# Message layers of a graph network: the node update's gate made inside the layer, its squares on ScalarE, its products last

## The reference

```python
def _block(h, src, dst, w, wm, bm, gm, bem, wu, bu, gu, beu, wg, bg):
    ecat = jnp.concatenate([h[src], h[dst]], axis=-1)
    em = jax.nn.relu(_layernorm(ecat @ wm.T + bm, gm, bem)) * w[:, None]
    msum = jax.ops.segment_sum(em, dst, num_segments=n)
    ...
    messages = msum / (cnt + 1e-08) * valid
    tw = jax.nn.sigmoid(h @ wg.T + bg)
    h_new = jax.nn.relu(_layernorm(jnp.concatenate([h, messages], axis=-1) @ wu.T + bu, gu, beu))
    return tw * h_new + (1 - tw) * h
```

## Time and profile before

| | us |
|---|---|
| median of 3 runs | 8488.0 (8477.32 to 8499.33) |
| profiled execution, its time | 8487.61 |
| profiled execution, its span | 8485.4 |
| busy: TensorE, VectorE, ScalarE, GpSimd | 5608.4, 3945.3, 3333.3, 4632.2 |

### The profile page before, as it was taken

The page is one execution under the profiler, slowest core; times in us unless marked ns, Lnnn a source line. Parts: engine busy times, 40 slices in busy tenths (PEclk is TensorE's granted clock), DMA queues, the critical chain, the costliest instruction groups (busy, mean ns, idle before and its releaser), DMA issues.

```text
span 8485.4 us, 124245 instructions
## 1 busy us (share of the span) xinstructions
PE 5608.4 (66%) x35700; PEld 4994.7 (59%) x35700; DVE 3945.3 (46%) x13716; ACT 3333.3 (39%) x12502; POOL 4632.2 (55%) x4868
## 2 busy tenths in 40 slices
PE   7445545577777667776757776675767775677676
PEld 5333333567666656666646666664666664666666
DVE  4221221456666556665653444452444443444445
ACT  2222221366666556666623333332333332333332
POOL 2555554366666356666526666535666663666662
PEclk9999999899999888888867888887888887888887
DMA  2011000334344234444313333333333332333332
GB/s 56 22 25 25 22 24 19 98 103 104 103 103 104 67 97 121 119 121 116 106 41 107 108 107 105 106 88 83 107 106 106 108 107 69 106 109 107 108 110 66
DMA packets 489685, 743.91 MB, mean 88 GB/s; under 512 B 219285, under 2 KB 351865, under 8 KB 487973
## 3 DMA queue, kind: packets, MB, share of 16 engines
q1 hardware_dynamic: 307764, 423.98, 16.0%
q0 software_dynamic: 180928, 305.59, 15.0%
q10 hardware_dynamic: 320, 6.40, 0.3%
HBM read 636.97 MB, written 97.83 MB: 87 GB/s over the span
## 4 chain that ended last, share of the span: by engine, by line
PE 20%; issue 14%; DVE 12%; another core or an unknown queue 12%; ACT 4%; DVEq 3%; ACTq 0%; POOL 0%; DMA 0%
PE PS L1355 5%; DVE AR L1943 5%; PE PS L1369 4%; PE PS L1245 2%; PE PS L1367 2%; PE PS L1269 2%; PE PS L1266 2%; DVEq L507 1%; ACT AR L1042 1%; DVE AR L1864 1%; PE PS L1380 1%; DVEq L1943 1%; DVE AR L1789 1%; ACT AR L1031 1%
## 5 line engine op out<-in xcount | busy, mean ns | idle before, releaser
L579 POOL DMA_INDIRECT AR<-gtab_d,AR x2436 | 2304.7, 946 | 1536.9 <-issue 606.2
L571 POOL DMA_INDIRECT AR<-ptab_d,AR x1624 | 1544.9, 951 | 1038.8 <-issue 394.1
L1042 ACT ACTIVATE AR<-PS,AR 128x512 f32<-128x512 f32 x609 | 418.2, 687 | 2533.9 <-remote 1286.9
L1355 PE MATMUL PS<-AR 128*112 128x132 f32 x4872 | 939.9, 334 | 673.3 <-DVE AR L1943 651.4
L1355 PEld LDWEIGHTS PS<-AR 128*112 128x112 f32 x4872 | 736.8, 211 | 819.0 <-DVE AR L1943 511.2
L1943 DVE TENSOR_TENSOR AR<-AR,PS 112x132 f32 x2436 | 696.1, 286 | 1002.3 <-issue 356.8
L553 POOL DMA_INDIRECT rec_d<-AR x782 | 756.9, 968 | 670.4 <-DVE AR L1550 446.4
L1369 PE MATMUL PS<-AR 128*128 128x128 f32 x4872 | 1051.8, 318 | 18.4 <-issue 18.2
L2020 DVE SCALAR_TENSOR_TENSOR AR<-PS,AR 128x512 f32<-128x512 f32 x609 | 455.7, 748 | 1211.9 <-issue 654.2
L1369 PEld LDWEIGHTS PS<-AR 128*128 128x128 f32 x4872 | 920.5, 235 | 20.6 <-issue 20.4
L1245 PE MATMUL PS<-AR 128*112 128x161 f32 x3248 | 667.9, 333 | 361.4 <-DVE AR L1864 218.4
(11 more groups left out here) (342 smaller groups left out, 8859.4 us busy)
## 6 DMA issues: line engine op xcount, KB each, us to landing
AR<-ste_d SPq DMA_DIRECT2D x404, 512.0 KB
AR<-nbb_d SPq DMA_DIRECT2D x303, 224.0 KB
ste_d<-AR SPq DMA_DIRECT2D x101, 512.0 KB
AR<-gtab_d,AR POOLq DMA_INDIRECT x2436
AR<-ptab_d,AR POOLq DMA_INDIRECT x1624
nbb_d<-AR SPq DMA_DIRECT2D x101, 224.0 KB
AR<-key_d SPq DMA_DIRECT2D x94, 224.0 KB
AR<-rec_d SPq DMA_DIRECT2D x812, 8.0 KB
```

The costliest lines, as they stand in the source:

```text
L571: e.indirect_dma_start(out=XJ1[:, t % 32, :], out_offset=None, in_=tabs_d[0][:, :], in_offset=off).then_inc(done_, 16)
L579: e.indirect_dma_start(out=xj2(t)[:, t % 4, :], out_offset=None, in_=tabs_d[1][:, :], in_offset=off).then_inc(done_, 16)
L1355: x = e.matmul(PS[6 + v_ % 2][0:B, (t % 2) * 132:(t % 2 + 1) * 132], SQ4[:, i % 4, t % 4, :], PX[:, i % 5, t % 4, :, :].rearrange("p c h - ...
```

## The change

- **Gate inside the layer.** `GATES` is the quad of the last own block plus 4 (169, 180). There ScalarE takes one exponential over all 28 blocks' gate columns of `Z`; two quads later VectorE makes the gate `tw33` and `n33` = 1 - gate; from four quads later on ScalarE multiplies `H` in place by 1 - gate, two blocks in each quad.
- **Update.** VectorE combines 160 columns instead of 161 (`updated`). ScalarE squares each block with an accumulator (`squares`) and takes the quarter's root (`update_root`). `mixed(l, q)`: reciprocal, times gate, seven instructions (times scale times gain), seven (plus bias times gate), one pass (clip and add the gated old features).
- **Order.** TensorE: updated 0 to 3, then products 0 to 3. ScalarE: the same, with squares of quarters 0, 1, 2, 3 beside updated 1, updated 2, products 0, products 1, and in layer 1 all row roots behind the last product. VectorE: updated 0, updated 1, mixed 0, updated 2, mixed 1, updated 3, mixed 2, mixed 3, then all `rows_out`.

```diff
 OWN = [{30 + 5 * b: b for b in range(NB)}, {122 + 2 * b: b for b in range(NB)}]
+
+GATES = [max(o) + 4 for o in OWN]
...
+                    if j == GATES[l]:
+                        w.wait_ge(s_dve, DV[f"own{l}"])
+                        done(e.activation(tw33, Z[:, :, D], ACT.Exp, scale=-1.0), s_act)
+                    lo = 2 * (j - GATES[l] - 4)
+                    if 0 <= lo < NB:
+                        w.wait_ge(s_dve, DV[f"om{l}"])
+                        for b in (lo, lo + 1):
+                            x = e.activation(H[:, b, :], H[:, b, :], ACT.Copy, scale=n33[:, b:b + 1])
+                        if lo + 2 == NB:
+                            done(x, s_act)
...
-                def roots(q):
-                    lo = q * CH
-                    done(root(ssq33[:, lo:lo + CH], 1.0 / D, f"us{l}_{q}"), s_act)
-                    tc = tw33[:, lo:lo + CH]
-                    done(e.activation(tc, U[:, lo:lo + CH, D], ACT.Exp, scale=-1.0), s_act)
...
-                def updated(q, norm_of=None, roots_of=None):
-                    for k in range(CH):
-                        sums_turned(q * CH + k)
-                        if k == 2 and roots_of is not None:
-                            roots(roots_of)
-                        if l == 1 and norm_of is not None:
-                            if k == 2:
-                                norm_root(norm_of)
-                            if k == 5:
-                                row_root(norm_of)
+                def squares(q, k):
+                    b = q * CH + k
+                    w.wait_ge(s_dve, DV[f"us{l}_{q}"])
+                    done(e.activation(SQ[:, b, :], U[:, b, 0:D], ACT.Square, accum_out=ssq33[:, b:b + 1]))
+
+                def update_root(q):
+                    x = ssq33[:, q * CH:(q + 1) * CH]
+                    w.wait_own()
+                    done(e.activation(x, x, ACT.Sqrt, bias=eps[0:B, :], scale=1.0 / D), s_act)
...
-                        done(e.activation(Z[:, q * CH + k, 0:n], PS[(2, 2, 2, 5)[q] + BANK[k]][0:B, PLACE[k] * n:(PLACE[k] + 1) * n], ACT.Copy), s_aev)
...
+                        done(e.activation(Z[:, q * CH + k, 0:n], PS[(2, 5, 2, 5)[q] + BANK[k]][0:B, PLACE[k] * n:(PLACE[k] + 1) * n], ACT.Copy), s_aev)
...
+                def with_squares(turn, q, of, k0):
                     for k in range(CH):
-                        b = q * CH + k
-                        turn_block("tab1" if l == 0 else "out", b, b % 2, HT1, HT2, True)
-                        if k == 4:
-                            products_out(q, (0, 1, 2))
-                            if roots_of is not None:
-                                roots(roots_of)
-                        if l == 1 and norm_of is not None:
-                            if k == 2:
-                                norm_root(norm_of)
-                            if k == 5:
-                                row_root(norm_of)
-                    products_out(q, (3, 4))
-                    products_out(q, (5, 6))
-
-                updated(0)
-                updated(1, roots_of=0)
-                products(0, roots_of=1)
-                updated(2, norm_of=0)
-                products(1, roots_of=2)
-                updated(3, norm_of=1)
-                products(2, roots_of=3)
-                products(3, norm_of=2)
+                        turn(q, k)
+                        if of is not None and k >= k0:
+                            squares(of, k - k0)
+                    if of is not None:
+                        for k in range(CH - k0, CH):
+                            squares(of, k)
+                        update_root(of)
+
+                def updated(q, k):
+                    sums_turned(q * CH + k)
+
+                def products(q, k):
+                    b = q * CH + k
+                    turn_block("tab1" if l == 0 else "out", b, b % 2, HT1, HT2, True)
+                    if k == 4:
+                        products_out(q, (0, 1, 2))
+                    if k == 6:
+                        products_out(q, (3, 4))
+                        products_out(q, (5, 6))
+
+                with_squares(updated, 0, None, 0)
+                with_squares(updated, 1, 0, 2)
+                with_squares(updated, 2, 1, 2)
+                with_squares(updated, 3, None, 0)
+                with_squares(products, 0, 2, 0)
+                with_squares(products, 1, 3, 2)
+                with_squares(products, 2, None, 0)
+                with_squares(products, 3, None, 0)
                 if l == 1:
-                    norm_root(3)
-                    row_root(3)
+                    for q in range(4):
+                        x = n33[:, q * CH:(q + 1) * CH]
+                        w.wait_ge(s_dve, DV[f"on{q}"])
+                        done(e.activation(x, x, ACT.Sqrt), s_act)
+                        done(root(ssq33[:, q * CH:(q + 1) * CH], 1.0 / 128, f"x{q}_0"), s_act)
...
                 updated(0, 2)
                 updated(1, 5)
                 w.wait_ge(s_dve, DV[f"us{l}_0"])
+                updated(2, 2)
+                w.wait_ge(s_dve, DV[f"us{l}_1"])
+                updated(3, 5)
+                w.wait_ge(s_dve, DV[f"us{l}_2"])
                 products(0, 2)
-                w.wait_ge(s_dve, DV[f"us{l}_1"])
-                updated(2, 5)
+                w.wait_ge(s_dve, DV[f"us{l}_3"])
+                products(1, 5)
                 w.wait_ge(s_aev, aev_at(p, CH - 1))
-                products(1, 2)
-                w.wait_ge(s_dve, DV[f"us{l}_2"])
-                updated(3, 5)
+                products(2, 2)
                 w.wait_ge(s_aev, aev_at(p, 2 * CH - 1))
-                products(2, 2)
-                w.wait_ge(s_dve, DV[f"us{l}_3"])
                 products(3, 5)
...
-            def update(l, q):
+            def updated(l, q):
 
                 lo = q * CH
-                Uz, Hc, tc = U[:, lo:lo + CH, 0:D], H[:, lo:lo + CH, :], tw33[:, lo:lo + CH]
-                w.wait_own()
                 for ks in ((0, 1, 2), (3, 4), (5, 6)):
                     w.wait_ge(s_mmu, sum_at(l, lo + ks[-1]))
                     for k in ks:
                         b = lo + k
-                        v(e.scalar_tensor_tensor(U[:, b, :], PS[(2, 5, 5, 5)[q] + BANK[k]][0:B, PLACE[k] * 161:(PLACE[k] + 1) * 161],
-                                                 CR[:, b:b + 1], Z[:, b, :], ALU.mult, ALU.add))
-                w.wait_own()
-                sumsq(Uz, SQ[:, lo:lo + CH, :], ssq33[:, lo:lo + CH], f"us{l}_{q}")
-                inverse(ssq33[:, lo:lo + CH], f"us{l}_{q}")
-                w.wait_ge(s_act, AC[f"tw{l}_{q}"])
-                v(e.tensor_scalar(tc, tc, 1.0, None, ALU.add))
-                w.wait_own()
-                v(e.reciprocal(tc, tc))
-                w.wait_own()
-                v(e.tensor_tensor(Uz, Uz, each(ssq33, lo, D), ALU.mult))
-                w.wait_own()
-                v(e.tensor_tensor(Uz, Uz, over(guB), ALU.mult))
-                w.wait_own()
-                v(e.tensor_tensor(Uz, Uz, over(beuB), ALU.add))
-                w.wait_own()
-                v(e.scalar_tensor_tensor(Uz, Uz, 0.0, Hc, ALU.max, ALU.subtract))
-                w.wait_own()
-                v(e.tensor_tensor(Uz, Uz, each(tw33, lo, D), ALU.mult))
-                w.wait_own()
-                mile(e.tensor_tensor(Hc, Hc, Uz, ALU.add), f"h{l}_{q}")
+                        x = e.scalar_tensor_tensor(U[:, b, 0:D], PS[(2, 5, 2, 5)[q] + BANK[k]][0:B, PLACE[k] * 161:PLACE[k] * 161 + D],
+                                                   CR[:, b:b + 1], Z[:, b, 0:D], ALU.mult, ALU.add)
+                        if k == 6:
+                            mile(x, f"us{l}_{q}")
+                        else:
+                            v(x)
+
+            def mixed(l, q):
+
+                lo = q * CH
+                Uz, Hc, sc = U[:, lo:lo + CH, 0:D], H[:, lo:lo + CH, :], ssq33[:, lo:lo + CH]
+                inverse(sc, f"us{l}_{q}")
+                v(e.tensor_tensor(sc, sc, tw33[:, lo:lo + CH], ALU.mult))
+                w.wait_own()
+                for b in range(lo, lo + CH):
+                    v(e.scalar_tensor_tensor(U[:, b, 0:D], U[:, b, 0:D], ssq33[:, b:b + 1], guB, ALU.mult, ALU.mult))
+                for b in range(lo, lo + CH):
+                    w.wait_ge(s_vown, w.count[s_vown.name] - CH + 1)
+                    v(e.scalar_tensor_tensor(U[:, b, 0:D], beuB, tw33[:, b:b + 1], U[:, b, 0:D], ALU.mult, ALU.add))
+                w.wait_own()
+                w.wait_ge(s_act, AC[f"hs{l}"])
+                mile(e.scalar_tensor_tensor(Hc, Uz, 0.0, Hc, ALU.max, ALU.add), f"h{l}_{q}")
...
+                    if j == GATES[l] + 2:
+                        w.wait_ge(s_act, AC[f"tw{l}"])
+                        v(e.tensor_scalar(tw33, tw33, 1.0, None, ALU.add))
+                        w.wait_own()
+                        v(e.reciprocal(tw33, tw33))
+                        w.wait_own()
```

(22 more changed lines are left out.)

18 lines of the change are left out of this document (7 added, 11 removed), and 4 rows, old and new, of the table DV.

## The result

| | before | changed |
|---|---|---|
| median of 5 runs, us | 8488.0 (8477.32 to 8499.33) | 8436.19 (8427.01 to 8441.27) |
| profiled execution, its time and span, us | 8487.61, 8485.4 | 8427.01, 8424.8 |
| busy: TensorE, VectorE, ScalarE, GpSimd, us | 5608.4, 3945.3, 3333.3, 4632.2 | 5601.5, 3907.3, 3352.0, 4643.3 |

The account below looks back on a forecast made before the run. Layers paced by gathers and slot return, updates by the order of TensorE, ScalarE and VectorE. Gains 27.6 (layer 0) + 22.2 (layer 1) - 1.2 (uncovered copies) = 48.6 us; 8487.6 - 48.6 = 8439.0 us, range 8410 to 8466.

Parts of the forecast that it names:

- Update 0: Layer 0's update, TensorE's first turn to last product copied out: 55.2 us instead of 82.8, a gain of 27.6 us.
- Update 1: Layer 1's update, TensorE's first turn to last output row: 98.6 us instead of 120.8, a gain of 22.2 us.
- The wait: Update of layer 1: VectorE stands some 4.3 us for the first row root, which ScalarE gives only behind all products.
- the term that carries layer 0's times over: Layer 1's update starts 1389.8 us after layer 0's, same steps; 128-column products save 0.4; quarter 3's features at 4294.7.
- Squares on ScalarE: Both updates: a square with accumulator costs 0.42 to 0.5 us, hidden by TensorE's own 0.74 us a block.
- The tail of layer 1: From 4211.6 ScalarE runs without a gap; gated copies of quads 196 and 197 lie there and cost 1.2 us.
- The stall at the start of layer 1: Behind layer 0's update TensorE is busy 8.7 of 43 us; gather 1 to gather 33 stays 71 us.
- rivals 3, 4 and 5: In order, stall after updates: takes gain back, 8488 us, chance 0.09; doubles, 8525, chance 0.04; shrinks by half, 8396, chance 0.07.
- Rival 1: Message layers pay for the work moved into them, 25 us if cover fails everywhere: 24.8 us gained, 8463; chance 0.10.
- rival 2: VectorE's block instructions in the updates are dear: 8442 us in its small form, 8462 at 0.6 us each; chance 0.05.
- rival 6: ScalarE becomes the updates' limit at 1 us a block instead of 0.71, 7 us more a layer: 8453; chance 0.10.
- A sign of being wrong that came true: In the update, VectorE idle between its quarters longer than 2 us after the second would show the forecast wrong.

Follow-up runs that it names:

- the two copies a quad: Changed kernel with two extra 128x160 ScalarE copies in each of quads 20 to 159 of both message layers; 8362.2 us (one run), changed kernel beside it 8372.4.
- the kernel with whole passes: Changed kernel with VectorE's 14 block instructions of a quarter made as four passes over the whole quarter; 8451.7 us (one run).

## Why the prediction was right

- **Update 0, 27.6 us forecast, 28.0 measured.** Its steps held too. New part of a quarter 5.95, measured 6.0 (block instruction 0.29 taken, 0.297 found). Roots of quarters 2 and 3 ready 34.7 and 42.5 us after the first turn, measured 34.2 and 41.9. Features 48.6, measured 48.0. Last products 6.6, measured 6.8.
- **Update 1, 22.2 forecast, 24.5 measured.** The wait (4.3 against 4.20) and the rows (11.53 against 11.58 a quarter) were right. Mis-sized is the term that carries layer 0's times over: features came 4255.13-4209.11 = 46.0 us after the first turn, not 48.2. That term holds a clock: the sums of the first quarter, some 42 matmuls, take 8.6 us in update 0 at a granted clock of 0.65, 7.5 in update 1 at 0.77, and 6.0 in the one trace in which update 0 ran at 1.00 from the start. Behind them the clock is 1.00 up to the features in all three, and the rest takes 39.4, 38.6 and 39.4 us. So of the 2.2 us about 1.1 are the clock, which was not forecast: luck. Another 0.6 is layer 0's own (48.0 for 48.6). The last 0.4 lies behind the first quarter, where layer 1 was 0.8 shorter and 0.4 was taken for its narrower products; what made it twice as much is not shown.
- **Squares on ScalarE**, 0.42 to 0.5 forecast: 0.44 in a block, 0.32 from start to start in a row. Hidden, as said; on VectorE they cost 6 us a layer as built.
- **The layers pay little or nothing** (at most the 2 to 3 us of one comparison). A gated copy takes 0.413 us and a pair 0.73, where 0.31 and 0.62 were worked out, and it didn't matter, because the cover is 2.2 us a quad. The tail of layer 1, from the last wait of ScalarE to the first turn, grew from 34.91 to 35.54 us: 0.6, not 1.2.
- **The stall at the start of layer 1** stayed (71.4 to 70.3 us), so rivals 3, 4 and 5 fell with the changed kernel's trace. Rival 1 fell with the two copies a quad, rival 2 with 0.297, rival 6 with 0.75 us a block.
- **A sign of being wrong that came true:** I named idle time of VectorE between its quarters of more than 2 us after the second. It was 2.85 us ahead of quarter 2's root. The mechanism doesn't fall with it, for my own sum held a longer wait: quarter 0 done at 2877.3, then 2.14, 5.95 and 2.14 us of work, and the root at 2891.4 leave about 3.9 us. The sign was drawn tighter than the sum.
- **Slips that carried no weight:** 3.65 us for a root is quarter 1's wait alone; the others waited 0.37, 1.24 and 1.25. The sums end at 2883.4 by the terms given, not 2883.6. The row of 348 ns set beside 324 ns is one of 128 elements, not 160. Behind the wait for the first row root stand 43.6 us of rows by the sum itself, not 46.
- **Where the reading was wrong without harm:** I said that a layer is paced by its gathers and the loop that gives back their slots. TensorE's waits over the middle of layer 0, kernel before and changed kernel, and then over the like stretch of the kernel with squares on VectorE, on the other chip:

```profile
PE PS L1229 <- issue: 133.7, 77, 3.2
...
PE PS L1234 <- issue: 137.4, 77, 3.1
PE PS L1234 <- DVE AR L1793: 13.5, 9, 3.1
```

```profile
PE PS L1270 <- DMA AR<-ptab_d,AR: 64.0, 103, 1.8
PE PS L1230 <- DVE AR L1788: 6.8, 14, 0.9
```

  In 600 us TensorE stood 133.7 and 137.4 us ahead of one line for nothing the profile names, and GpSimd waited for it; on the other chip that idle time is gone, TensorE waits for the gathers, and these come every 1.27 us. So in the forecast's traces TensorE's unexplained waits held back the gathers. The conclusion that ScalarE has room stood on its own idle time, and that was right.

## What to carry to other kernels

- In a stage where three engines hand work round, shortening the work and loosening the order are no separate gains. Either alone moved the bound to the other (71 and 74 us of 83); both together took 28 us off. Forecast them as one schedule, from the first instruction to the last, and not as a sum.
- Work that needs no result of a stage belongs ahead of it, where another resource sets the pace. How much fits is at most the idle time of that engine in a cycle (here 2.2 us of 6), and a few dummy instructions measure it: 0.7 us went in free, of 2.66 only some 1.5.
- When work is moved behind everything else, look at what then waits first. One reduction and one root moved forward gave 4.6 us of it back.

## What the runs showed of the hardware

- The same kernel took 6783 us on one chip and 8422 to 8504 on another. GpSimd's gather is 0.95 us on both. The attention part, first gather to last, took 3227 and 3977 us. The difference in a layer is idle time: TensorE is busy 436.5/393 = 1.11 us for each gather on the slow chip and 523.8/478 = 1.10 on the quick one (squares on VectorE, 1400 to 2000 us), and idle 0.42 and 0.16. Most of that idle time is marked as issue and comes in pieces, 77 of them in those 600 us, 1.8 us on average and at most 3.1. What it is stays open: no run here was made to tell.
- TensorE's granted clock is part of what an update costs. Before, 340 matmuls in 82.8 us at 0.79 took 58.9 us of busy time; in the changed kernel they took 49.1 at 0.95, and 46.4 us in the trace with 1.00. A count of instructions does not show this part. At the end of the path it can be read alone: the last quarter's 46 matmuls of products with their copies took 9.4 us at 0.67 before, behind 6.92 us of idle time, 8.5 at 0.80 in the kernel with whole passes, and 6.8 at 1.00 in the changed kernel, so 2.7 of the 28 us lie there. The rest of its share no run here separates.
- Two table loads of ScalarE with only a root between them cost 1.28 us each, and the next instruction starts 1.29 to 1.30 us behind the load's start, as the rows of the gate in the update show. The Trainium skill (ScalarE: Activation LUTs, "What ACT_TABLE_LOAD costs") counts 2.66 us for an exchange with its drain; no row here has one.
